# The decayed queries of a delta-rule block made on GpSimd instead of VectorE

## What is computed

```
f = x @ Wf1 @ Wf2;  log_f = log_sigmoid(f)        # a decay for each token and channel
q = silu(x @ Wq);   k = l2norm(silu(x @ Wk));  k_ = -2*sigmoid(x @ Wbeta) * k
for each token:                                    # two steps, the second with k, v, q
    S = exp(log_f) * S + (k_ * exp(log_f)) (k . S)
    S = S + k_ (k . S) + k v
    o = q . S
```

## Time and profile before

| | |
|---|---|
| median of 3 runs | 2699.11 us |
| the profiled execution | 2707.01 us, of it 2705.2 us from its first to its last instruction |
| granted TensorE clock, mean | 0.940 |
| TensorE matmuls busy | 2298.0 us, 85% |
| VectorE busy | 1605.1 us, 59% |
| ScalarE busy | 1629.6 us, 60% |
| GpSimd busy | 459.2 us, 17% |
| DMA queue of SyncE | 47.1% of 16 engines' span |

### The profile page before, as it was taken

One profiled execution on the slowest core, in us unless ns is written; L12 is line 12 of the kernel. 1 busy time (PEld: TensorE's weight loads), 2 busy tenths in 40 slices (PEclk: granted clock), 3 DMA queues, 4 the chain that ended last, 5 costly groups with the idle time before them and its releaser, 6 DMA issues.

```text
span 2705.2 us, 224996 instructions
## 1 busy us (share of the span) xinstructions
PE 2298.0 (85%) x102472; PEld 1742.0 (64%) x102472; DVE 1605.1 (59%) x3940; ACT 1629.6 (60%) x3048; POOL 459.2 (17%) x555
## 2 busy tenths in 40 slices
PE   4778878988888898888889888888988888888875
PEld 2466656666666666666667666666666666666664
DVE  2455356655666665566666556666655666665543
ACT  2555445666666666666666666666665666666544
POOL 1011111111111111111111111111211111121110
PEclk8789789999999999999999999999999999999887
DMA  3334443455555445555544555554445555444541
GB/s 76 84 102 109 112 124 102 123 141 141 146 131 139 117 123 136 142 144 140 138 118 123 133 138 142 144 136 121 122 134 137 140 144 134 130 120 121 134 121 49
DMA packets 692946, 339.10 MB, mean 125 GB/s; under 512 B 551794, under 2 KB 651728, under 8 KB 692816
## 3 DMA queue, kind: packets, MB, share of 16 engines
q1 hardware_dynamic: 692816, 337.67, 47.1%
HBM read 35.57 MB, written 16.78 MB: 19 GB/s over the span
## 4 chain that ended last, share of the span: by engine, by line
PE 77%; issue 10%; DVE 7%; DMA 4%; ACT 1%; SPq 0%; DVEq 0%; ACTq 0%
PE bank L562 14%; PE bank L716 10%; PE bank L695 9%; PE bank L687 9%; PE bank L707 6%; PE bank L585 4%; PE bank L699 4%; PE bank L667 4%; PE bank L614 4%; DMA uq_a<-uqv 4%; PE bank L569 2%; PE bank L629 2%; DVE uqv L1253 2%; PE bank L594 2%; PE bank L579 2%
## 5 line engine op out<-in xcount | busy, mean ns | idle before, releaser
L469 POOL TENSOR_TENSOR state<-moved,edge 128x512 f32<-128x512 f32 x252 | 292.6, 1161 | 1891.5 <-DVE moved L1069 1891.5
L834 ACT ACTIVATE parts<-bank,cf 128x256 f32<-128x256 f32 x512 | 215.1, 471 | 363.6 <-DVE o_col L1063 358.0
L695 PE MATMUL bank<-parts,w_now 32*32 32x64 f32 x16512 | 414.5, 221 | 5.7 <-DMA w_now<-w_row 2.9
L562 PE MATMUL bank<-x_col,w_kqv 128*128 128x512 f32 x768 | 376.3, 634 | 37.1 <-issue 36.4
L699 PE MATMUL bank<-aq_now,delta 32*32 32x16 f32 x16512 | 398.4, 178 | 5.2 <-issue 5.2
L699 PEld LDWEIGHTS bank<-aq_now,delta 32*32 32x32 f32 x16512 | 386.5, 109 | 2.1 <-issue 2.1
L695 PEld LDWEIGHTS bank<-parts,w_now 32*32 32x32 f32 x16512 | 373.4, 110 | 18.1 <-issue 5.9
L716 PE MATMUL bank<-uq_now,s_now 32*32 32x24 f32 x32768 | 360.3, 188 | 18.7 <-issue 18.6
L716 PEld LDWEIGHTS bank<-uq_now,s_now 32*32 32x32 f32 x32768 | 334.1, 106 | 29.5 <-issue 23.0
L1063 DVE TENSOR_TENSOR o_col<-qs,bank 128x64 f32<-128x64 f32 x512 | 89.7, 217 | 431.6 <-PE bank L699 427.8
L1092 DVE COPY_PREDICATED aq<-ci,bank 128x128 f32<-128x128 int32 x256 | 77.1, 301 | 434.2 <-PE bank L687 358.7
(11 more groups left out here) (99 smaller groups left out, 3801.6 us busy)
## 6 DMA issues: line engine op xcount, KB each, us to landing
s_now<-state SPq DMA_DIRECT2D x256, 256.0 KB, 2.7
uq_now<-uqv SPq DMA_DIRECT2D x256, 192.0 KB, 2.6
t_now<-t_t SPq DMA_DIRECT2D x256, 128.0 KB
w_now<-w_row SPq DMA_DIRECT2D x256, 128.0 KB
uq_a<-uqv SPq DMA_DIRECT2D x64, 384.0 KB
low<-uqv SPq DMA_DIRECT2D x64, 384.0 KB
x_col<-in_xt_dram SPq DMA_DIRECT2D x32, 512.0 KB, 3.7
w_a<-w_col SPq DMA_DIRECT2D x64, 256.0 KB
```

Source lines behind the costliest of these rows:

```text
L469: pool.tensor_tensor(state[:, qc, :, :, :].rearrange("p m b v -> p (m b) v"), moved[m % 2][:, :, :, :].rearrange("p m b v -> p (m b) v"), ...
L562: mm = pe.matmul(ps[:, :], w_kqv[:, a, w, f * P:(f + 1) * P], x_col[:, a, :], start=a == 0, stop=a == KT - 1)
L695: pe.matmul(ds_bank[quarter(h), m, :, :].rearrange("p b v -> p (b v)"), w_now[quarter(h), m, :], parts[quarter(h), m, :, :].rearrange("p b ...
L834: act.activation(parts[:, :, b, :], p2_bank, ACT.Copy, scale=cf[:, C_TAKE + b:C_TAKE + b + 1])
```

## The change

The two products q leave VectorE's stream. GpSimd does them between its decay of slot 6 and its decay of slot 7, after waits for `ep`, for the queries and for the last DMA that reads the old content of `uqv`. Each of them counts up `q_ready`, so that SyncE waits for two counts. Operands, layout and arithmetic stay as they are.

```
-        q_ready = signal("q_ready", 1)
+        q_ready = signal("q_ready", HF)
...
-                        u_made, q_made = held(sp, first, u_ready.at(j + 1, 1)), held(sp, second, q_ready.at(j + 1, 1))
+                        u_made, q_made = held(sp, first, u_ready.at(j + 1, 1)), held(sp, second, q_ready.at(j + 1, HF))
...
+            def query_products(j, c):
+
+                if there(j + 2):
+                    pool.wait_ge(ep_ready.handle, ep_ready.at(j + 2, 1))
+                    pool.wait_ge(drained["q"].handle, drained["q"].at(j + 2, HF))
+                    if there(j):
+                        pool.wait_ge(uq_in.handle, uq_in.at(j, 16 * CH))
+                    for f in range(HF):
+                        pool.tensor_tensor(by_token(uq_of(uqv[c], f), RQ, slice(ROWS, RQ)),
+                                           tokens_of(q_col[:, f, :]), slots_of(ep, f, 1),
+                                           ALU.mult).then_inc(q_ready.handle, 1)
...
                 for n in range(4, CH):
+                    if n == CH - 1:
+                        query_products(j, c)
                     decay_part(j, c, n)
...
                     last.then_inc(u_ready.handle, 1)
-                    dve.wait_ge(drained["q"].handle, drained["q"].at(j + 2, HF))
-                    for f in range(HF):
-                        last = dve.tensor_tensor(by_token(uq_of(uqv[c], f), RQ, slice(ROWS, RQ)),
-                                                 tokens_of(q_col[:, f, :]), slots_of(ep, f, 1), ALU.mult)
-                    last.then_inc(q_ready.handle, 1)
```

## The result

| | before | after |
|---|---|---|
| median of 4 runs | 2699.71 us | 2731.11 us |
| lowest and highest | 2698.57, 2705.89 | 2722.25, 2739.11 |
| ratio | | 1.0111, 95% interval 1.0071 to 1.0150 |
| the profiled execution, its span | 2705.2 us | 2733.3 us |
| granted TensorE clock, mean | 0.940 | 0.931 |

The change made the kernel slower by 1.1%, some 30 us. The forecast was 9 us slower (2708 us), with a range that ended at 2722. In the code of after, the lines of TensorE, ScalarE and VectorE stand 14 higher than before: o_col is 1077, w_col 1247, u 1267, the scores 701. GpSimd's new products are line 482.

The account below looks back on a forecast made before the run. TensorE was taken to wait for the staging issued behind q. Per group 2.08 us of blocking less 0.62 cover less 1.20 saved gave +0.26; 26 groups plus two early ones made 9 us, 2708 us, range 2690 to 2722.

Parts of the forecast that it names:

- What bounds: Turn from slot 7 to slot 0: TensorE's scores wait for the staging DMA, issued after q; 27 waits, 90.5 us.
- What is taken away: End of slot 7: the two products q leave VectorE's path, so the staging is issued 1.20 us earlier per group.
- The meeting: Slot 6: GpSimd's products and VectorE's w block each other; VectorE loses D - 0.20 each, 2.08 us for two.
- D: Length of one GpSimd product q, 512 elements by 512 with no operand repeated; taken as 1.24 us.
- rival of faster: At w: GpSimd's products do not stop VectorE, or only one does; up to -31 us, about 2669, or 2679; chance 0.15.
- rival of break-even: Same mechanism at w, with D near the decay's 1.05 us: -2 us, 2697; chance 0.29.
- The cover: Behind w, before slot 7's o_col: VectorE's wait for TensorE hides 0.62 us of the delay per group.
- The sum: Staging issue per group: 2.08 less 0.62 less 1.20 = +0.26 us; with two early groups, 9 us slower.
- What else comes later, and why it costs nothing: Slots 7 and 0: deltas start some 0.3 us late, qs and t_t about 1.1, all inside TensorE's 2.87 us of idling.
- The range: Whole kernel: 2690 to 2722 us, for D from 1.05 to 1.45 plus some margin for the cover and the 0.20.
- The gross gain: TensorE's wait ahead of slot 0's scores: 1.20 us back in each of 26 groups, 31 us, if nothing else moved.
- rival 2: Faster, at w: GpSimd's products do not stop VectorE, or only one does; up to -31 us, about 2669; chance 0.15.

Follow-up runs that it names:

- e1_gate: The changed kernel, with GpSimd's two products q also waiting until VectorE's products w are done; 2702.93 us, ratio 1.0008.
- e8_one_each: The changed kernel with one product q on GpSimd and the other on VectorE, behind the products u; 2705.56 us, ratio 1.0014.
- e2_gate_busy: e1_gate plus six statistics of 256 elements on VectorE behind the products w, delaying slot 7 without a meeting; 2735.08 us, ratio 1.0129.
- e9_gate_busy4: e2_gate_busy with four statistics on VectorE instead of six; 2705.50 us, ratio 1.0020.
- e10: The kernel before with four unread matrix products on TensorE ahead of each group's first scores; 2707.00 us, ratio 1.0029.
- e11: e1_gate with three unread matrix products on TensorE ahead of each group's first scores; 2689.80 us, ratio 0.9970.
- e4: The changed kernel, but GpSimd's products go to r_col, unread then, and VectorE does the products q as before; 2764.48 us, ratio 1.0221.
- e5: The kernel before with six unread matrix products on TensorE ahead of each group's first scores; 2705.74 us, ratio 1.0007.
- e3: The kernel before with one transpose of 128 elements on VectorE ahead of the products q; 2704.44 us, ratio 1.0000.

## Why the prediction was right and wrong

**What bounds.** Right: the staging is on the path, and TensorE waited for it 27 times after as before (88.8 us in all, before 90.5).

**What is taken away.** 1.20 us forecast. From o_col to the issue it is now 5.49 us (1330.99 to 1336.48) and was 6.76 (1324.44 to 1331.20): 1.27.

**The meeting, and D.** Right. D measured 1.20 us (e1_gate) for 1.24, w took 4.50 where the sum gave 4.57, and two meetings cost 2.01 for 2.08; one cost 1.01 (e8_one_each). The rule of the Trainium skill's page "SBUF — State Buffer" (the section "Who interferes with whom") is borne out in both directions: two tiles from SBUF on VectorE's side block (w in the change, 4.50 us for 2.49), one does not (o_col and moved in e1_gate). The prediction's rival of faster falls. So does the premise of its rival of break-even, a D below 1.17; but the outcome that this rival had for the sum is about what came.

**The cover.** About right: o_col starts 4.42 us behind the start of w, before 1324.44 - 1321.36 = 3.08; 1.34 us later for 1.46.

**The sum.** +0.26 us per group forecast, +0.07 measured in the group shown (+0.18 in the next, +0.11 on average), and an iteration with the clock as in the kernel before takes 78.3 to 78.8 us, then 78.3 to 78.7. So as far as it went, the sum was rather too high, and what it covered would have been a draw.

**"What else comes later, and why it costs nothing."** This is the step that failed. I had TensorE's start of deltas, ScalarE's t_t and qs swallowed by TensorE's 2.87 us of idling, took TensorE's pace as given, and let the staging take the same 3.6 us from issue to scores. Deltas did start 0.4 us late inside the idling, and in the iterations at the old clock that cost nothing, as forecast. The profile of before had the warning: clock 0.940 on average, the scores behind the idling at 2.78 us for 128 matmuls, where the 128 of the next pair take 1.56 later in the iteration. I never priced that difference, 1.2 us in each group, nor asked what sets it off: in the group of the earlier trace rows the clock falls at 1334.89, just as the scores start, after 2.87 us without work. In the change this fall is twice as long in 11 of 25 iterations, and a second one comes in slot 4 in 13. That is 36 us in the 25 iterations. e2_gate_busy shows that the delay brings it on without any meeting; its iterations and the change's show that this happens where the staging also takes 4.4 us from issue to scores (10 of the 11 in the change, all 8 in e2_gate_busy). In e9_gate_busy4, where o_col is 0.7 us late and no scores start more than 6.5 us behind `deltas`, 2 of 25 iterations lose it that way. No run has slot 7 late by the full 1.3 us with the scores no later than before, or the slower way with nothing late and the issue where it was, so which of the two counts for how much is not shown.

**The range.** It took in D and the cover and no change of pace, so its top at 2722 was 9 us too low for the median. The chances leaned the right way: 0.56 for slower.

**The gross gain.** I had it at 31 us, and the prediction's rival 2 was built on that. e1_gate puts it to the test and finds next to nothing: of 25 us in 25 iterations slot 0 keeps 9, since in every other group the staging is used no sooner, and slot 4 with its lower clock takes 10. That the total came out level is a balance of the two, not a sign that the staging does not matter.

What stays open: by what the fall in slot 4 is brought on, some 40 us behind the scores. It came more often when slot 0 ran at full speed (e10, e11: 20 of 25) and when slot 7 was late (after: 13; e4: 17); no experiment changed slot 4 itself. Also open is why the way from the staging's issue to the scores alternates between 3.6 and up to 4.8 us in the kernels that issue it behind u and not behind the products q; the kernel before (3.6 and up to 3.9) has a trace of it. The counts of iterations are from one execution each.

## What to carry to other kernels

Work moved to GpSimd is not parallel to VectorE while both read SBUF tiles in pairs (w took 4.50 us for 2.49); put it beside VectorE's instructions that take one operand from PSUM, as e1_gate does. Where TensorE idles in every iteration and its clock falls behind that, a delay that seems covered by the idling need not be free, and a gain there need not be kept in full: price the clock with the windows of the stages behind, and widen the range by it. Compare iterations, not only means: one length against two in turn told more here than any sum.

## What the runs showed that I had not expected

Keeping TensorE at work ahead of the scores kept the clock at 2.4 GHz there in all 25 iterations and shortened slot 0 by 1.0 to 1.3 us, and yet gained nothing, since slot 1 was 0.4 us longer and slot 4 then fell to 1.2 GHz in 13 (e5) and 20 (e10) of them, for 1.2 us each. The time at 1.2 GHz can fall by half (85 to 44 us) with no gain. In e10 the iterations with no fall at all last 77.6 us, 0.9 less than before, those with one in slot 4 last 78.8, 0.2 more. A fall in slot 4 thus cost 1.1 us, and being rid of the one in slot 0 won 0.9, with the longer slot 1 counted in. And 0.2 us of delay (e3) changed nothing that can be measured, where 1.3 (e2) cost 1.3%.
